# One core, eight image pairs of attention and a top-2 expert layer: the opening reordered, four placements moved inside a pair

## What is computed

```
tokens = patchify(x)                 # 256 tokens of 320 numbers per image
h  = tokens @ W ; h = layernorm(h) * gamma
xn = layernorm(h)
q, k = silu(xn@Wq), silu(xn@Wk) ; v = xn@Wv        # 16 heads of 64
cum = cumsum(-softplus(xn@Wa + ba))                # per head, over tokens
attn = (q k^T) * exp(cum_i - cum_j), causal
o = groupnorm(attn v) * sigmoid(xn@Wg)
h = h + o @ Wo
h = h + top-2-of-8 experts(layernorm(h))           # gelu, hidden size 1024
```

## Time and profile before

| | |
|---|---|
| median of 3 executions | 1319.3 us (1314.68 to 1319.67) |
| profiled execution | 1316.64 us, of it 1314.6 us span |
| PE busy | 1251.5 us (95%) |
| ACT / DVE / POOL busy | 858.2 / 824.6 / 425.4 us |
| TensorE clock granted, mean | 0.986 of full |
| first pair's first `scores` / first `weighted` | 48.29 / 52.63 us |
| opening: embedding weights in, first embedding on PE | 7.2 us, 7.25 to 12.2 us |
| opening: SP issues Wq, Wg | 2.97 us, 13.78 us |
| one `weight_hi` (ACT) / `weight_lo` (DVE) | 1.9 / 2.3 us |
| in a pair: `decay` (ACT) / `spread` / two norms (DVE) | 1.5 / 0.77 / 0.73 us |
| pairs 0 to 7, attention | about 48 to 828 us; one pair about 101 us |
| expert blocks | to the end |

### The profile page before, as it was taken

How to read it: one execution, slowest core, us unless ns; L and a number is a source line. 1 busy time by engine, 2 the same in 40 slices (tenths; PEclk the granted TensorE clock), 3 DMA queues, 4 the chain that set the end, 5 groups by cost and what they waited for, 6 DMA issues and landing times. The chain is left out here.

```text
span 1314.6 us, 27299 instructions
## 1 busy us (share of the span) xinstructions
PE 1251.5 (95%) x8534; PEld 1072.4 (82%) x8534; DVE 824.6 (63%) x2120; ACT 858.2 (65%) x2019; POOL 425.4 (32%) x524
## 2 busy tenths in 40 slices
PE   6799999999999999999999999999999999999996
PEld 4576877877877877878878768889899999989996
DVE  4456466566666566665665566657788888555562
ACT  3567567667567567576576465637788888666662
POOL 2111211241241241241241132154445544434433
PEclk8899999999999999999999899999999999999998
DMA  5423222242231341341331335468987886888883
GB/s 185 143 100 90 78 91 88 77 129 74 93 122 55 110 132 49 116 131 47 114 116 56 101 95 193 151 186 245 278 232 220 230 242 184 250 271 269 251 239 83
DMA packets 125607, 194.46 MB, mean 148 GB/s; under 512 B 16272, under 2 KB 91504, under 8 KB 125360
## 3 DMA queue, kind: packets, MB, share of 16 engines
q1 hardware_dynamic: 110864, 175.37, 41.5%
q0 software_dynamic: 13584, 17.26, 6.4%
q10 hardware_dynamic: 1056, 0.55, 0.2%
HBM read 167.40 MB, written 29.05 MB: 149 GB/s over the span
## 5 line engine op out<-in xcount | busy, mean ns | idle before, releaser
L1190 PE MATMUL bank<-xn_sp,big_r 128*128 128x512 f32 x1152 | 315.2, 411 | 2.2 <-DVE big_r L1694 1.7
L1190 PEld LDWEIGHTS bank<-xn_sp,big_r 128*128 128x128 f32 x1152 | 206.6, 190 | 56.4 <-issue 2.4
L837 ACT ACTIVATE dec_x<-dec_x,ncum 128x256 f32<-128x256 f32 (+1 forms) x512 | 189.7, 444 | 10.4 <-POOL dec_x L663 10.4
L1717 DVE TENSOR_TENSOR att<-bank,dec_x 128x384 f32<-128x384 f32 x256 | 130.6, 552 | 102.7 <-PE bank L1229 100.8
L663 POOL TENSOR_SCALAR_AFFINE_SELECT dec_x<-dec_x 128x256 f32<-128x256 f32 x256 | 101.7, 427 | 225.2 <-DMA dec_x<-cum_scratch 224.9
L1535 PE MATMUL bank<-big_r 128*128 128x256 f32 x1296 | 168.0, 286 | 1.9 <-ACT mid_f L907 1.3
L1535 PEld LDWEIGHTS bank<-big_r 128*128 128x128 f32 x1296 | 160.5, 192 | 3.6 <-ACT mid_f L907 1.7
L714 POOL TENSOR_SCALAR mid_f<-mid_f,dec_x 128x256 f32<-128x256 f32 x71 | 77.5, 1096 | 184.7 <-DVE mid_f L1968 182.3
L720 POOL DMA_INDIRECT out<-mid_f,tok x71 | 117.8, 1660 | 53.7 <-POOL mid_f L714 20.2
L1984 DVE TENSOR_TENSOR big_r<-mid_f,big_r 128x256 fp32r<-128x256 f32 x216 | 91.2, 423 | 69.5 <-ACT big_r L927 69.5
L907 ACT ACTIVATE mid_f<-bank,h 128x256 f32<-128x256 f32 x216 | 101.3, 478 | 43.9 <-PE bank L1535 21.6
(11 more groups left out here) (231 smaller groups left out, 2224.5 us busy)
## 6 DMA issues: line engine op xcount, KB each, us to landing
big_f<-in_L_ffn_w SPq DMA_DIRECT2D x68, 1024.0 KB, 6.4
dec_x<-cum_scratch SPq DMA_DIRECT2D x128, 384.0 KB, 3.5
big_w<-in_L_ffn_w SPq DMA_DIRECT2D x12, 1024.0 KB, 6.4
mid_f<-expert_rows SPq DMA_DIRECT2D x27, 261.0 KB, 3.2
h<-h_scratch SPq DMA_DIRECT2D x8, 512.0 KB, 4.6
out<-h SPq DMA_DIRECT2D x16, 256.0 KB, 4.0
xt<-in_x SPq DMA_DIRECT2D x15, 256.0 KB, 3.8
h_scratch<-h SPq DMA_DIRECT2D x15, 256.0 KB, 2.6
```

Source lines behind the costliest of these rows:

```text
L837: act.activation(d, d, ACT.Exp, bias=ncum[p % 2][:, NS * u + s, 2 * c + hh:2 * c + hh + 1]).then_inc(M["exp_done"], 1)
L1190: mm = pe.matmul(bank[target][:, :], wp[:, k, c * P:(c + 1) * P], xp[:, k, :], start=(k == 0 and j == 0), stop=(k == EC - 1 and j == 2))
L1717: dve.tensor_tensor(att[hh][:, :], bank[4 + hh][:, 0:LW], dec[n % RING][:, hh, :], ALU.mult).then_inc(M["mult_done"], 1)
```

## The change

SP's opening waits for the patches of image 1 and the embedding weights before it issues the big weight loads, and stores the running sums and loads the decay rows before it stores h. Image 1's side buffers move to `h2` and `xn2` (the wait on h_out in `keep_v` goes). ACT's, PE's and DVE's openings are reordered. In every pair: `keep_o(p, 6)` goes to the head of ACT's last step, `softplus` to the head of step 5, `turn(2p+2)` with `keep_xnT` and `scaled_h` to the end of step 1, and on DVE `normed` and `spread` ahead of `silu_q` in step 5; in step 3 `embed_norm(2p+3)` and the first `y_lo` swap places. The number of instructions of each kind stays.

```diff
@@ -164,8 +164,6 @@
         xn1 = turned[:, :].rearrange("p (s n) -> p s n", s=NS)
         xn2T = turned[:, :].rearrange("p (k n) -> p k n", k=EC)
         xs = sb("xs", [P, EC, SP2])
-        h2 = sb("h2", [P, TP, E])
-        xn2 = sb("xn2", [P, TP, EW])
         cumT = sb("cumT", [TP * H, P])
         ccs = sb("ccs", [P, TP * H])
         ncum = [sb(f"ncum{i}", [P, TP, H]) for i in range(2)]
@@ -181,11 +179,13 @@
         rs1 = sb("rs1", [P, 2, NS])
         eps0 = sb("eps0", [P, NS])
         pick = sb("pick", [P, TP, TOPK, X])
+        h2 = sb("h2", [P, TP, E])
+        xn2 = sb("xn2", [P, TP, EW])
 
 
         side_x = [xt, mid_f[:, 2048:2048 + (KT + 1) * S].rearrange("p (k n) -> p k n", k=KT + 1)]
-        side_h = [h1, mid_f[:, 2816:3328].rearrange("p (s n) -> p s n", s=NS)]
-        side_n = [xn1, mid_f[:, 3328:3840].rearrange("p (s n) -> p s n", s=NS)]
+        side_h = [h1, h2[:, 0:NS, :]]
+        side_n = [xn1, xn2[:, 0:NS, 0:E]]
         little = pick[:, :, :, :].rearrange("p t k n -> p (t k n)")
         side_st = [st1, little[:, 0:6].rearrange("p (s k) -> p s k", s=NS)]
         side_su = [st1u, little[:, 6:12].rearrange("p (s k) -> p s k", s=NS)]
@@ -454,17 +454,19 @@
 
             load_patches(0)
             load_patches(1)
+            sp.wait_ge(M["wt_in"], 32)
+            sp.wait_ge(M["xt_in1"], 32)
             load_weight(0)
             load_weight(1)
             load_patches(2)
             load_weight(2)
             load_weight(3)
-            store_h(0)
-            store_h(1)
             store_cum(0)
             for c in range(2):
                 for u in range(2):
                     load_decay(0, c, u)
+            store_h(0)
+            store_h(1)
             load_weight(4)
 
             def ahead(p, c, u):
@@ -824,7 +826,6 @@
                 have(act, "o_ps", 2 * NP * (p - 1) + (2 * GC if n == 0 else 2 * NP))
                 if p == 0 and t >= NS and n == 0:
                     act.wait_ge(M["tok_ps"], 2)
-                    act.wait_ge(M["h_out"], 32)
                 act.activation(v_sb[:, t, n * 512:(n + 1) * 512], bank[source][:, :], ACT.Copy).then_inc(M["v_done"], 1)
 
             def decay(p, c, u):
@@ -928,11 +929,12 @@
 
             def last_step(p):
                 main, nxt = pair(p), pair(p + 1)
+                if main:
+                    keep_o(p, 6)
                 if nxt:
                     xn_hi(p + 1)
                 if main:
                     y_hi(p, 0, 0)
-                    keep_o(p, 6)
                     if p == NPR - 1:
                         x_early(0)
                     y_hi(p, 0, 1)
@@ -961,6 +963,8 @@
                     keep_xnT(2 * p + 3)
                 if c == 6 and post:
                     keep_x2(2 * p - 2)
+                if c == 5 and nxt:
+                    softplus(p + 1)
                 if main:
                     tanh_q(p, c + 1)
                     decay(p, c + 1, 0)
@@ -970,8 +974,6 @@
                     affined(p - 1, 1, c - 1)
                 if c == 3 and post:
                     y_hi(p - 1, 1, 1)
-                if c == 5 and nxt:
-                    softplus(p + 1)
                 if c == 6 and main:
                     affined(p, 0, 0)
                 if main:
@@ -985,9 +987,6 @@
                 if c == 0 and routed:
                     top_exp(2 * p - 4)
                     top_exp(2 * p - 3)
-                if c == 1 and nxt:
-                    keep_xnT(2 * p + 2)
-                    scaled_h(2 * p + 2)
                 if c == 2 and post:
                     y_hi(p - 1, 1, 0)
                 if c == 3 and nxt:
@@ -998,6 +997,9 @@
                     affined(p, 0, 1)
                 if main:
                     tanh_g(p, c + 1)
+                if c == 1 and nxt:
+                    keep_xnT(2 * p + 2)
+                    scaled_h(2 * p + 2)
 
             weight_hi(0)
             weight_hi(1)
@@ -1005,17 +1007,18 @@
             weight_hi(2)
             keep_xnT(1)
             xn_hi(0)
+            weight_hi(3)
             softplus(0)
+            tanh_q(0, 0)
+            keep_v(0, 0, 2)
+            keep_cum(0)
+            for i in range(1, TP):
+                keep_v(0, i, 2 + i)
+            tanh_k(0, 0)
+            tanh_g(0, 0)
             scaled_h(0)
             scaled_h(1)
-            tanh_q(0, 0)
-            keep_cum(0)
-            weight_hi(3)
-            for i in range(TP):
-                keep_v(0, i, 2 + i)
             decay(0, 0, 0)
-            tanh_k(0, 0)
-            tanh_g(0, 0)
             decay(0, 0, 1)
             for p in range(NPR):
                 for c in range(NP):
@@ -1418,8 +1421,6 @@
                     keys(p, c + 1)
                 if c == 0 and post:
                     gn_var(p - 1, 1)
-                if c == 1 and nxt:
-                    turn(2 * p + 2)
                 if c == 1 and main:
                     values(p, 5, 0, "sq_done", NP * p + 3)
                 if c == 2 and main:
@@ -1434,6 +1435,8 @@
                     turn2(2 * p - 1, "lg_done", 2 * p - 1)
                 if main:
                     gates(p, c + 1)
+                if c == 1 and nxt:
+                    turn(2 * p + 2)
                 if c == 3 and nxt:
                     turn(2 * p + 3)
                 if c == 4 and post:
@@ -1454,11 +1457,11 @@
             turn(1)
             logits(0)
             queries(0, 0)
+            cum(0)
             values(0, 0, 2, "s1_xnT", 2)
+            cum_rows(0)
             values(0, 1, 3, "s1_xnT", 2)
-            cum(0)
             values(0, 2, 4, "s1_xnT", 2)
-            cum_rows(0)
             values(0, 3, 5, "s1_xnT", 2)
             keys(0, 0)
             gates(0, 0)
@@ -2027,6 +2030,11 @@
                 if main:
                     if c > 0:
                         head_stats(p, c - 1)
+                if c == 5 and post:
+                    normed(2 * p - 2)
+                if c == 5 and main:
+                    spread(p, 0)
+                if main:
                     silu_q(p, c + 1)
                 if c == 0:
                     if post:
@@ -2037,13 +2045,8 @@
                     embed_norm(2 * p + 2)
                 if c == 2 and routed:
                     place(p - 2)
-                if c == 3 and post:
-                    y_lo(p - 1, 1, 0)
-                if c == 5:
-                    if post:
-                        normed(2 * p - 2)
-                    if main:
-                        spread(p, 0)
+                if c == 3 and nxt:
+                    embed_norm(2 * p + 3)
                 if c == 6:
                     if nxt:
                         running_sums(p + 1)
@@ -2075,9 +2078,8 @@
                     if nxt:
                         embed(2 * p + 3)
                 if c == 3:
-                    if nxt:
-                        embed_norm(2 * p + 3)
                     if post:
+                        y_lo(p - 1, 1, 0)
                         y_lo(p - 1, 1, 1)
                 if c == 4 and nxt:
                     decay_logits(p + 1)
@@ -2103,9 +2105,9 @@
             decay_logits(0)
             weight_lo(1)
             log_decay(0)
-            weight_lo(2)
             running_sums(0)
             silu_q(0, 0)
+            weight_lo(2)
             weight_lo(3)
             silu_k(0, 0)
             dve.wait_ge(M["g_in"], 16 * 7)
```

## The result

Device microseconds, one core. The changed kernel took 1286.7 us (median of 4 executions, 1284.18 to 1290.23), the kernel before 1318.7 us beside it (4 executions, 1314.68 to 1319.67): a ratio of 0.9765, 95% interval 0.9733 to 0.9796, 32.0 us less. The prediction was 1291.6 us in a range of 1286 to 1303: direction right, gain underestimated by 7 us, the median inside the range near its lower end.

What follows compares the result with a forecast made beforehand. PE, busy 95% of the span, was taken to bound the kernel outside the opening, itself a chain of waits. Pairs 17.5 us plus opening 7.5 made 25.0 us off 1316.6: 1291.6 us, range 1286 to 1303.

Steps and rivals of the forecast that it cites:

- (a): Opening: small constants no longer share queues with 2 MB, so the first embedding chain starts 2.5 to 3.3 us earlier.
- (b): Opening: first big weight load goes out near 7 us instead of 3, costing 0 to 1.5 us; last in at 24.
- (c): Opening, ACT: weight_hi(3) stands ahead of softplus, which still ends about 28.1 us instead of 31.09.
- (d): Opening: PE does cum and cum_rows around one values group; keep_cum ends 31 to 32 us, a gain of 5.5 us.
- (e): Opening: from the sums' stores to the first mask stays 7.54 us; the first mask ends at about 39.6.
- (f): Opening: tanh_k, tanh_g and both scaled_h precede ACT's first exponentials; first weighted at 42.7 us, gain 10 us.
- against it stands the clock: Opening: PE's idle pieces bring one or two half-speed stretches on the path, costing 1.7 to 5 us, taken as 2.5.
- The restarts: Pairs: groups that no longer wait start before the one ahead has ended, gaining 1.5 us in all (0 to 2).
- The first: Rival, opening: gives little because Wg arrives 5 us late or PE runs it at the low level; 1298 us, chance 0.15.
- the fourth: Rival, whole kernel: no effect because the trace's waits were modelled ends of matmuls; 1310 to 1316 us, chance 0.02.
- The third: Rival, step 5: softplus waits for decay_logits and blocks q and k of heads 6; 1331 us, chance 0.02.
- The second: Rival, pairs: give half, as waits return under another name or pair 6's clock still falls; 1301 us, chance 0.13.

Runs made afterwards that it cites:

- the second execution of the changed kernel: The changed kernel run once more, unedited, beside the runs of its opening alone and its pairs alone: 1287.1 us, ratio 0.9765.
- the run with filling matmuls: The kernel before plus twelve matmuls with unused results ahead of the waiting group in pair 6's last step: 1317.3 us against 1319.4, ratio 0.9987.
- without the hold: The changed kernel without SP's two waits ahead of the big weight loads: 1290.1 us, ratio 0.98 on the kernel before.
- the two halves: The kernel before with only the opening's edits, 1308.8 us, ratio 0.9924; and with only the pairs' edits, 1299.7 us, ratio 0.986.
- `softplus` and the norms: The kernel before with softplus at the head of ACT's step 5 and normed and spread ahead of silu_q on DVE: 1311.4 us against 1317.6, ratio 0.9958.

## Why the prediction was right, and where it was off

**What bound the kernel**: right. Each wait forecast to go went, and the other engines' busy times moved by 1.2 us at most. The gain was 7.3 us larger than forecast (32.3 against 25.0 in the profiled executions), and it divides so.

**Opening, +1.8 us.** The steps came out nearly as put: (a) statistics 2.7 us earlier (2.5 to 3.3); (b) last weight in at 22.3 us (24), the hold cost nothing; (c) `softplus` ends at 27.2 (28.1); (d) stores at 32.1 (31 to 32); (e) 7.51 us (7.54), the first mask starts at 39.6 (forecast: over at 39.6); (f) first `weighted` 43.17 (42.7), 9.5 us earlier instead of 10. By the first `weighted` the forecast was 42.7 and 2.5 for the clock, 45.2 us, and 43.17 were measured: the forecast came 2.0 us too late (1.8 counted at the first `scores`), and two terms share it. The larger is in the chain (c) to (f), which was put too slow. In the second execution of the changed kernel, where PE's part of this chain ran at full clock, `softplus` ended at 27.1 (28.1), the stores went out at 30.35 us (31 to 32) and the first `weighted` came at 41.03 instead of 42.7: 1.7 us. The smaller is "against it stands the clock". One low stretch on the path came in the first execution and cost 2.1 us against the second, where I took 2.5; in the second none came, so which of the two one gets is luck. The windows view gives both openings, before and then after:

```profile
18.00:53.00 35.00, 25.34 (x101) 19.64 (x103) 17.36 (x27) 17.67 (x31) 4.46 (x10) 0.76 0.37 127
```

```profile
18.00:44.00 26.00, 21.79 (x98) 16.50 (x97) 15.18 (x22) 17.97 (x31) 3.48 (x8) 0.87 0.36 137
```

A mean of 0.76 over 35 us is 17 us at the low level, 0.87 over 26 us is 7. The 10 us of (f) are counted from the old chain as it was measured, with its low stretches in it, so only the new one's had to be charged; but the forecast did not see that the new opening would have fewer of them. Eight executions with the old opening start `scores` between 47.1 and 50.3 us, five with the whole new one or its opening half between 36.7 and 39.4 (one of these with h's stores first): about 11 us apart in the mean, so the opening is worth more than the 7.5 forecast and the 9.3 of the first execution.

**Pairs 0 to 5, +2.1 us.** The waits were worth what their rows said. Two small terms were off. The costs of the turn's move and of pair 0's `weight_lo`, 0.6 each here, measured 0 in pairs 1 to 5 and 0.4 us in pair 0 (step 2, with the turn alone and in the changed kernel): 0.8 us too much. The restarts, 1.3 here, were sized too low: the norm's swap gave 0.95 for a wait of 0.77, and pair 0 gave 2.0 us around step 5 for waits of 1.0 and 0.5. That is the rest, 1.3 us, by subtraction.

**Pair 6**: 5.5 against 5.4 us, with both parts as worked out, 1.31 us of wait left, 0.52 before the q projection, and 2.5 us for the clock by the run with filling matmuls. The clock's part hangs on the execution before having had a full low stretch of 6.8 us there, which three of six executions with this wait had.

**Pair 7, +1.8 us.** The end of the pair was held by DVE's chain as forecast. The gain came at its start, from the wait of 1.95 us that became 1.69 and behind which the clock did not fall. I had costed no difference there. Most of it is luck of the clock: with the same edits the wait was 1.82, 1.86 and 2.04 us in three other runs (the pairs alone, without the hold, h's stores first), the level did fall, and pair 7 won 0.3, 0.3 and -1.1 us.

**Expert blocks, +1.5 us**: nothing shows them to be the change's. From the last `scores` to the end took 489.4 to 492.7 us in seven executions with the old last step and 487.0 to 493.7 in six with the new one, all with the expert blocks unedited. This pair of executions lay well.

**The rivals.** The first (the opening gives little) and the fourth (the waits are modelled) fell with the two halves. The third (slower, `softplus` late blocks q and k) did not happen in the change. The run with ACT's move alone shows the kind of thing it described, though: a wait under another name that eats the whole gain, on DVE and not in `scores`. The second (the pairs give half) fell too; the drain of the Trainium skill, which was one way to it, does not show.

## What to carry to other kernels

Read an in-order queue as a chain of its own: an operation that moves on one engine delays whatever stands behind its consumer on the next, so a move on ACT may need its partner on DVE; ACT's alone lost time here (DVE's alone was not run). Where the first result hangs on a small load, let the large loads wait for it; here that cost the last large load nothing. Where PE idles often, ask which low stretch of the clock would lie on the chain: the same kernel had its first result 2.1 us later in the execution in which one did. A gain that rests on the clock not falling needs several executions to be read.

## What was not expected of the hardware

**A wait's length alone did not decide the clock.** Behind pair 6's wait of 3.2 us the level fell in five of six executions: for 6.8 us in the execution before, with the opening alone and with `softplus` and the norms; for 3.4 us with `softplus` alone and with the norm's swap alone; and not at all with the turn alone. Timeline of that last kernel:

```profile
725.04 0.65 PE L1240 MATMUL bank<-att,mid_f 128*64 128x256 f32 x4 [3.20 <-ACT big_f L842]
```

Where that wait is 1.31 us (seven executions) the level never fell. Pair 7's wait of 1.7 to 2.0 us went with a low stretch in nine of thirteen executions (the execution before among them) and with none in both executions of the changed kernel, with `keep_o` alone (1.96 us) and with the turn alone (1.95 us). So the 2.6 us of pair 6 is what a low stretch of 6.8 us costs when it comes; where only 3.4 us came (`softplus` alone, the norm's swap alone), the cost was 1.6 us. With the wait of 1.31 us it was never paid. In the fourteen traces together, between 60 and 1270 us, every low stretch stands beside a wait of PE of 1.73 us or more, and none beside the 42 waits of 1.2 to 1.7 us. What else decides it stays open.

**Small loads behind large ones.** The same 16 KB landed in 11.3 us with the large loads ahead and in 5.4 us without.

**The expert blocks' scatter,** 3 to 7 us, is larger than most single edits here, and its cause stays open; no run was made for it.
